# Two PSUM banks for the side chain and two for the maxima's ring, in a planned four-network kernel

## The reference, cut to what matters

```python
# L0, non-local block: keys and values are 2x2 max-pooled, 256 of them
f = softmax(einsum('bcn,bcm->bnm', theta(x), pool(phi(x))))          # 1024 x 256
x = bn(conv1x1(einsum('bnm,bcm->bcn', f, pool(g(x))))) + x
# L1, wavelet block: Haar transform, 1x1 convolutions, spatial and channel gates
x = haar_inverse(relu(bn(proj(gates(relu(bn(fuse(haar(x))))))))) + x
# L2, attention with one head over 128 channels
q, k, v = conv1x1(group_norm(x))
alpha = softmax(einsum('bci,bcj->bij', q, k) * C ** -0.5)             # 1024 x 1024
x = x + conv1x1(einsum('bcj,bij->bci', v, alpha))
# L3, attention with eight heads of 16 channels, then a small MLP
q, k, v = split(einsum('oc,bchw->bohw', w_qkv, group_norm(x)))
attn = softmax(einsum('bhdi,bhdj->bhij', q, k) * temp)                # 8 x 1024 x 1024
x = x + conv1x1(einsum('bhdj,bhij->bhdi', v, attn))
x = x + mlp(group_norm(x))
```

## Time and profile before

| | |
|---|---|
| median of 3 runs | 1871.0 us (1866.97 to 1877.07) |
| profiled execution, own time / span | 1865.36 us / 1863.9 us |
| TensorE (PE) busy | 1565.3 us, 84% of the span |
| VectorE (DVE) busy | 1133.5 us, 61% |
| ScalarE (ACT) busy | 815.9 us, 44% |
| GpSimd (POOL) busy | 273.7 us, 15% |
| granted TensorE clock, mean | 0.871 of full speed |
| one full window (936 to 1149 us) | 213 us |

### The profile page before, as it was taken

The page is one execution under the profiler, slowest core; times in us unless marked ns, Lnnn a source line. Parts: engine busy times, 40 slices in busy tenths (PEclk is TensorE's granted clock), DMA queues, the critical chain, the costliest instruction groups (busy, mean ns, idle before and its releaser), DMA issues.

```text
span 1863.9 us, 20833 instructions
## 1 busy us (share of the span) xinstructions
PE 1565.3 (84%) x6466; PEld 695.4 (37%) x6466; DVE 1133.5 (61%) x1912; ACT 815.9 (44%) x1514; POOL 273.7 (15%) x305
## 2 busy tenths in 40 slices
PE   6579679898889989899889998799879989985982
PEld 3236325433443335333343335333343334332330
DVE  5454664766568584767568574776667574665601
ACT  1113202465327552465327552365326553752670
POOL 5004102110130103010130102201130103000000
PEclk6789957998889799899889799898899899976995
DMA  2000012011110303011120303003020203023001
GB/s 50 12 12 6 11 29 52 6 26 45 28 37 7 80 1 65 6 29 53 25 41 7 80 1 60 12 7 75 12 53 7 68 11 61 18 52 58 13 12 35
DMA packets 31569, 58.64 MB, mean 31 GB/s; under 512 B 14678, under 2 KB 16862, under 8 KB 31456
## 3 DMA queue, kind: packets, MB, share of 16 engines
q1 hardware_dynamic: 27296, 50.41, 12.6%
q0 software_dynamic: 4160, 6.83, 2.4%
HBM read 14.37 MB, written 4.50 MB: 10 GB/s over the span
## 4 chain that ended last, share of the span: by engine, by line
PE 52%; issue 20%; DVE 8%; DMA 6%; SPq 5%; ACT 4%; POOL 3%; POOLq 0%; ACTq 0%; DVEq 0%
PE ps L1337 52%; SPq L689 3%; DVE x L1189 3%; DVE mx L1283 3%; DMA invw<-inverse_sums 2%; DMA qp<-q3h 2%; POOL acc L849 2%; ACT p L1015 2%; SPq L666 1%; SPq L692 1%; POOL ogc L816 1%; DMA inverse_sums<-inv 1%; ACT hn L928 0%; DVE x L1196 0%; DVE x L1195 0%
## 5 line engine op out<-in xcount | busy, mean ns | idle before, releaser
L1283 DVE TENSOR_REDUCE mx<-ps 128x1 f32<-128x512 f32 x1024 | 648.8, 682 | 259.6 <-PE ps L1337 257.5
L1015 ACT ACTIVATE p<-ps 128x512 f32<-128x512 f32 x1024 | 550.7, 600 | 304.6 <-PE ps L1337 302.5
L1337 PE MATMUL ps<-kp,qp 63*128 63x512 f32 x1024 | 418.2, 512 | 85.2 <-DVE mx L1283 41.4
L1337 PE MATMUL ps<-qp,kp 64*128 64x512 f32 x1024 | 396.5, 478 | 22.5 <-ACT p L1015 17.7
L1337 PEld LDWEIGHTS ps<-qp,kp 64*128 64x128 f32 x1024 | 172.3, 198 | 330.0 <-ACT p L1015 233.5
L1337 PE MATMUL ps<-p,vt 128*32 128x512 f32 x2048 | 287.9, 635 | 6.5 <-ACT p L1015 6.2
L1337 PEld LDWEIGHTS ps<-kp,qp 63*128 63x128 f32 x1024 | 176.2, 206 | 216.8 <-DVE mx L1283 133.8
L980 ACT ACTIVATE p<-ps 128x512 f32<-128x512 f32 x128 | 76.2, 597 | 220.5 <-PE ps L1337 188.3
L1337 PE MATMUL ps<-p,vT 128*128 128x512 f32 x256 | 143.5, 654 | 0.7 <-ACT p L980 0.5
L849 POOL TENSOR_TENSOR acc<-acc,p 128x512 f32<-128x512 f32 x96 | 126.4, 1316 | 70.8 <-ACT p L980 67.3
L1279 DVE TENSOR_REDUCE mx<-ps 128x1 f32<-128x512 f32 x128 | 84.4, 683 | 39.1 <-PE ps L1337 39.1
(11 more groups left out here) (192 smaller groups left out, 1660.3 us busy)
## 6 DMA issues: line engine op xcount, KB each, us to landing
qp<-q3h SPq DMA_DIRECT2D x128, 64.0 KB, 2.9
xin<-in_x SPq DMA_DIRECT2D x8, 512.0 KB, 4.6
acc<-inverse_sums SPq DMA_DIRECT2D x16, 256.0 KB, 3.7
kp<-k3h POOLq DMA_DIRECT2D x64, 64.0 KB, 4.1
qp<-q3l SPq DMA_DIRECT2D x64, 64.0 KB, 3.2
x3a<-x SPq DMA_DIRECT2D x8, 512.0 KB, 4.7
kp<-k3h SPq DMA_DIRECT2D x64, 64.0 KB, 2.5
x3b<-x3a SPq DMA_DIRECT2D x8, 512.0 KB, 2.9
```

Source lines behind the costliest of these rows:

```text
L1015: a.activation(p3[:, s % 2, i, :], ps[:, SB + (u + 1) % 3, :], ACT.Exp).then_inc(sem("p3_ready"), 1)
L1283: v.tensor_reduce(mx3[:, i, c, h:h + 1], ps[:, bank, :], AX.X, ALU.max).then_inc(sem("mx3_ready"), 1)
L1337: return nc.tensor.matmul(o, l, r, start=start, stop=stop)
```

## The change

Three things change together. The maxima's ring in the windows has two banks in place of three (banks 0 and 1). The bank that it gives up, bank 2, becomes the side chain's second bank: `side_bank` gives half 0 to bank 7 and half 1 to bank 2. TensorE then issues both halves of a stage at one visit, and between stages waits for the half in question and not for both. The first part keeps its order (`alone`). The plan's tables are moved by a few laps (the first hunks below are of STEADY: the turns of the maxima, L0 on TensorE and on VectorE, Q2 and Q3 on ScalarE), and the first part gets filler matmuls in laps 9, 10 and 135.

```diff
-    "turned": {"DVE": (69, 87, 157), "PE": (71, 87, 157), "ACT": (71, 89, 158), "SP": (72, 90, 158)},
+    "turned": {"DVE": (69, 83, 157), "PE": (71, 87, 157), "ACT": (71, 88, 158), "SP": (72, 90, 158)},
...
-            "L0": {0: 107, 2: 110, 4: 111, 6: 114, 8: 118, 10: 119, 12: 122, 14: 126, 16: 130, 19: 135, 21: 138, 23: 142, 25: 146, 27: 152, 29: 155, 31: 156, 33: 157},
+            "L0": {0: 107, 2: 110, 4: 111, 6: 114, 8: 118, 10: 119, 12: 122, 14: 126, 16: 130, 19: 135, 21: 138, 23: 141, 25: 145, 27: 152, 29: 157, 31: 158, 33: 163},
...
-            "L0": {5: 111, 7: 114, 9: 117, 11: 119, 13: 122, 15: 126, 28: 152, 30: 155, 32: 157, 34: 158},
+            "L0": {5: 111, 7: 114, 9: 117, 11: 119, 13: 122, 15: 126, 28: 152, 30: 157, 32: 159, 34: 160},
...
-            "Q2": {4: 16, 6: 20, 8: 23, 10: 27, 12: 31, 14: 34, 16: 38},
-            "Q3": {4: 47, 6: 50, 8: 57, 10: 61, 12: 65, 14: 69, 16: 74},
+            "Q2": {4: 16, 6: 20, 8: 23, 10: 25, 12: 29, 14: 32, 16: 36},
+            "Q3": {4: 47, 6: 50, 8: 57, 10: 59, 12: 65, 14: 69, 16: 71},
...
-STEADY_PLAN = Plan(STEADY, (1, None, 0), 3)
-LAST_PLAN = Plan(LAST, (1, None, 0), 3)
+STEADY_PLAN = Plan(STEADY, (1, None, 0), 2)
+LAST_PLAN = Plan(LAST, (1, None, 0), 2)
...
+        def side_bank(at, k, first=XB):
+
+            return first if at.plan is FIRST_PLAN else (XB, MB + 2)[k % 2]
...
                 for name, w, n, before in ((q, wq, 5, None), (k, wk, 9, q)):
                     for h in range(NH):
-                        yield at(bt, stage, n + 2 * h)
-                        if h:
+                        alone = at.plan is FIRST_PLAN
+                        if alone or h == 0:
+                            yield at(bt, stage, n + 2 * h)
+                        if alone and h:
                             wait(pe, sem(name + "_split"), bt, NH, h)
                         elif before:
-                            wait(pe, sem(before + "_split"), bt, NH)
-                        else:
+                            wait(pe, sem(before + "_split"), bt, NH, NH if alone else h + 1)
+                        elif h == 0:
                             wait(pe, sem("h" + tag + "_ready"), bt)
-                        mm(ps[:, XB, :], w, half(hn, h)).then_inc(sem(name + "_ps"), 1)
+                        mm(ps[:, side_bank(at, h), :], w, half(hn, h)).then_inc(sem(name + "_ps"), 1)
...
                 for h in range(NH):
-                    yield at(bt, "L0", 27 + 2 * h)
-                    if h:
+                    if alone or h == 0:
+                        yield at(bt, "L0", 27 + 2 * h)
+                    if alone and h:
                         wait(pe, sem("inv0_ready"), bt, NH, h)
-                    else:
+                    elif h == 0:
                         wait(pe, sem("p0_added"), bt)
-                    mm(ps[:, bank_of(bt), :], ones[:], half(x1, h)).then_inc(sem("den0_ps"), 1)
+                    mm(ps[:, side_bank(at, h, MB + 2), :], ones[:], half(x1, h)).then_inc(sem("den0_ps"), 1)
                 for h in range(NH):
-                    yield at(bt, "L0", 31 + 2 * h)
-                    if h:
+                    if alone or h == 0:
+                        yield at(bt, "L0", 31 + 2 * h)
+                    if alone and h:
                         wait(pe, sem("x1_ready"), bt, NH, h)
                     else:
-                        wait(pe, sem("inv0_ready"), bt, NH)
+                        wait(pe, sem("inv0_ready"), bt, NH, NH if alone else h + 1)
                     for m in range(2):
-                        last = mm(ps[:, bank_of(bt), :], wg[:, m, :], half(p0[:, m, :], h), start=m == 0, stop=m == 1)
+                        last = mm(ps[:, side_bank(at, h, MB + 2), :], wg[:, m, :], half(p0[:, m, :], h), start=m == 0, stop=m == 1)
                     last.then_inc(sem("y0_ps"), 1)
...
```

More of the change, by code:

```diff
@@ L243 @@
     "fill": "000000000000000000000000000000000000000000000000000000000000000000000000000000000000000000000000000000000000000000000000000000000000000000000000000000000000000000000000000000000000",
-    "beside": 73,
+    "beside": 72,
 }
@@ L939, in queries @@
                         wait(act, sem(name + "_ps"), bt, NH, h + 1)
-                        a.activation(half(hi, h), ps[:, XB, :], ACT.Identity, bias=bias).then_inc(sem(name + "_hi"), 1)
+                        a.activation(half(hi, h), ps[:, side_bank(at, h), :], ACT.Identity, bias=bias).then_inc(sem(name + "_hi"), 1)
                 for h in range(NH):
@@ L955, in projections @@
                         wait(act, sem(name + "_ps"), bt, NH, h + 1)
[L956 removed]
+                        a.activation(half(hi, h), ps[:, side_bank(at, h), :], ACT.Copy, scale=scale).then_inc(sem(name + "_hi"), 1)
                 for h in range(NH):
@@ L1188, in non_local @@
                     wait(dve, sem("den0_ps"), bt, NH, h + 1)
-                    v.reciprocal(half(x1, h), ps[:, bank_of(bt), :]).then_inc(sem("inv0_ready"), 1)
+                    v.reciprocal(half(x1, h), ps[:, side_bank(at, h, MB + 2), :]).then_inc(sem("inv0_ready"), 1)
                 for h in range(NH):
@@ L1404, in non_local @@
                 wait(pe, sem("x_in"), bt, 16)
+                alone = at.plan is FIRST_PLAN
                 for h in range(NH):
-                    yield at(bt, "L0", 2 * h)
-                    if h:
+                    if alone or h == 0:
+                        yield at(bt, "L0", 2 * h)
+                    if alone and h:
                         wait(pe, sem("theta_ready"), bt, NH, h)
-                    mm(ps[0:CI, bank_of(bt), :], wth[:], half(xin, h)).then_inc(sem("theta_ps"), 1)
+                    mm(ps[0:CI, side_bank(at, h, MB + 2), :], wth[:], half(xin, h)).then_inc(sem("theta_ps"), 1)
                 for h in range(NH):
-                    yield at(bt, "L0", 4 + 2 * h)
-                    if h:
+                    if alone or h == 0:
+                        yield at(bt, "L0", 4 + 2 * h)
+                    if alone and h:
                         wait(pe, sem("pooled"), bt, NH, h)
                     else:
-                        wait(pe, sem("theta_ready"), bt, NH)
-                    mm(ps[:, bank_of(bt), :], wpg[:], half(xin, h)).then_inc(sem("phig_ps"), 1)
+                        wait(pe, sem("theta_ready"), bt, NH, NH if alone else h + 1)
+                    mm(ps[:, side_bank(at, h, MB + 2), :], wpg[:], half(xin, h)).then_inc(sem("phig_ps"), 1)
                 for k in range(4):
-                    yield at(bt, "L0", 8 + 2 * k)
-                    if k:
-                        wait(pe, sem("nm0_ready"), bt, 4, k)
-                    else:
+                    if alone or k % 2 == 0:
+                        yield at(bt, "L0", 8 + 2 * k)
+                    if k == 0:
                         wait(pe, sem("phi_ready"), bt, 2)
+                    elif alone or k >= 2:
+                        wait(pe, sem("nm0_ready"), bt, 4, k if alone else k - 1)
                     for c in (2 * k, 2 * k + 1):
-                        last = mm(ps[:, bank_of(bt), M0 * (c % 2):M0 * (c % 2 + 1)], part(th, c), phz[:])
+                        last = mm(ps[:, side_bank(at, k, MB + 2), M0 * (c % 2):M0 * (c % 2 + 1)], part(th, c), phz[:])
                     last.then_inc(sem("s0max_ps"), 1)
@@ L1495, in wavelet @@
                 for k in range(4):
-                    if k % 2 == 0:
+                    alone = at.plan is FIRST_PLAN
+                    if k == 0 or alone and k == 2:
                         yield at(bt, "L1", 13 + k)
-                        if k:
-                            wait(pe, sem("pj_ready"), bt, 4, k)
-                        else:
-                            wait(pe, sem("chout_ready"), bt)
-                    last = mm(ps[:, XB, Q * (k % 2):Q * (k % 2 + 1)], part(wpr, k), chout[:])
+                    if k == 0:
+                        wait(pe, sem("chout_ready"), bt)
+                    elif alone and k == 2:
+                        wait(pe, sem("pj_ready"), bt, 4, k)
+                    last = mm(ps[:, side_bank(at, k // 2), Q * (k % 2):Q * (k % 2 + 1)], part(wpr, k), chout[:])
                     if k % 2:
@@ L1557, in tail @@
                 for h in range(NH):
-                    yield at(bt, "TL", 2 * h)
-                    if h:
-                        wait(pe, sem("x4_ready"), bt, NH, h)
-                    else:
+                    if h == 0:
+                        yield at(bt, "TL", 2 * h)
                         wait(pe, sem("yn_ready"), bt)
@@ L1564, in tail @@
                         wait(pe, sem("xo_ready"), bt + -1, NH)
-                    mm(ps[:, XB, :], wo[:], half(ogc, h)).then_inc(sem("o3_ps"), 1)
+                    mm(ps[:, side_bank(at, h), :], wo[:], half(ogc, h)).then_inc(sem("o3_ps"), 1)
                 yield from group_averages("TL", 4, bt, grp4, "4", mv4, ps[:, XB, 0:1], ps[:, XB, 1:2])
@@ L1573, in tail @@
                 for h in range(NH):
```

(8 more changed lines are left out.)

73 lines of the change are left out of this document (38 added, 35 removed), and 10 rows, old and new, of tables (FIRST, LAST, STEADY).

## The result

The changed kernel takes 1979.82 us (median of 4 runs, 1976.51 to 1982.78); the kernel before beside it 1868.99 (4 runs). The ratio is 1.060, interval 1.0569 to 1.0631: 111 us slower. The profiled execution of after took 1976.51, its span is 1974.9, its mean granted clock 0.874 (before: span 1863.9, 0.871).

A forecast was written before the change was run, and what follows sets the result against it. TensorE was taken to set the pace, with the three-bank ring's latency at its limit in each burst. 100 - 20 - 11 + 10 + 4 + 17 = +100 on 1865.36 gave 1965, forecast as 1971 us at the median; range 1878 to 2070.

The forecast's parts named there:

- The burst: Heads, burst without side work: with two banks the fourth maxima tile starts 0.60 us late, so 2.73 becomes 3.33 us.
- 154 bursts at 0.65 = 100: Heads: 154 bursts between value products each pay 0.65 us for the two-bank ring, 100 us in all.
- The 28 bursts that were taken off: Heads: of 182 bursts, 28 (four a window) were held free of loss because paired side visits cover the wait.
- the bound: Heads: upper limit of the ring's price, 182 bursts at 0.75 us, 137 us.
- What the pairs cost, +10: Two halves at one visit fill the wait for ScalarE once, not twice: 0.4 us more per pair, +10 us.
- their waits, -11: Side chain: TensorE's waits for v's copies and k's low parts go, and some in the last tail: -11 us.
- End of L0, -20: Ends of five windows: both sums come at once, the next window begins 4 us sooner, -20 us.
- The one wait for a reciprocal that was to stay before y: End of L0: of TensorE's waits for L1189, all were to go but one before y.
- Moved visits, +4: STEADY laps 27, 34 and 61: ScalarE's earlier reads of k and v delay exponentials, +4 us.
- Clock, +17: Heads before L0 begins: in half of six windows four bursts stay at half clock, +17 us.
- The rival in which the clock falls for good: Heads: gaps of 0.6 us keep half of the 154 bursts at half clock, 2050 to 2080 us; chance 0.2.
- The third bank is not needed: Rival, heads: the 0.60 runs beside ScalarE's wait at the fourth score tile, only pairs count, 1845 us; chance 0.09.

The follow-up runs named there:

- the ring alone: The kernel before with only the windows' maxima ring cut from three banks to two, side chain and tables kept: 2072.37 us, ratio 1.1118.

## Why the prediction was right, and which of its terms were not

The direction, the mechanism and the total were right: slower by 111 us where 100 were forecast, 1979.8 against 1971. The total owes something to luck: errors of both signs cancel in it.

- *The burst.* Right. 3.31 us came where 3.33 was worked out, with the third tile 0.06 after the reduction two places before. A visit after tile 2 does cover the wait, as the pair of 4.25 us shows.
- *154 bursts at 0.65 = 100.* Too small for the ring alone, which costs 208 us, 161 of them in the heads. The 28 bursts that were taken off are covered by pairs, so the ring alone stands against 182 x 0.65 = 118. The prediction priced a burst with a visit between tiles 3 and 4 at 0.75 and kept it for the bound; it is 0.83 to 0.85 in the table of the four bursts, and such bursts are common. The third stretch of a window pays 2.8, for side work in front of a reduction, which had no term. Up to about 47 of the 161 us can be clock. In the kernel after, the heads and the step between them cost 109 us in all.
- *Attention part.* A term that was missing. The ring runs into VectorE's wavelet block earlier: +27 us in the profile. Moving two tiles gives 21 us back, but a like move gives the kernel before 17. The bursts in the prediction were counted in the heads only.
- *What the pairs cost, +10, and their waits, -11.* The net of the two was forecast at about nothing, and with the -20 at L0's ends all pairs stood at -21. The runs give -82: L0's ends are 25 us below the kernel before and 33 below the ring alone, and in the heads the pairs give 41 back, some of the 82 by the clock. The step reckoned the pairs against bursts of three banks, where a half fills the wait for ScalarE. In the ring of two banks a half after tile 3 hides 0.13 us of itself, and a pair after tile 2 nearly 1 us: 3.31 + 1.94 (a pair ahead of the tiles: 5.25 - 3.31) - 4.25 = 1.00.
- *End of L0, -20.* Right in size: -22 in the profile, in five windows. The one wait for a reciprocal that was to stay before y did not: at the window's end TensorE now waits for the ring and the turn, and the 9.7 us for L1193 lie in the first part.
- *Moved visits, +4.* Wrong sign, small: the tables together give about 10 us back. In five windows the pair moved to lap 141 gives 0.8 each, 4 in all.
- *Clock, +17.* Not seen as a loss of its own: the mean is 0.874 against 0.871. The rival in which the clock falls for good is out. The first group of heads, at 1.00 before in windows 0 to 6, is at 1.00 after in windows 1 to 6; in the one of 65.7 us it has nine recorded gaps of 0.19 to 1.12 us. What the Trainium skill tells of a bf16 kernel ("TensorE: Matmul & The Clock Gate", section "A second HAM failure mode: psum-queue depth-cycling"), that small idle gaps send the clock back and forth, is therefore not borne out in these groups of the kernel after. The ring alone comes nearer to it: in windows 0 to 5 the same groups fall to 0.50 once, for 3.4 to 13.6 us, and its mean over the span is 0.850. The first part, where the prediction saw agreement, stays at 0.50 for 35 us and does not go back and forth.
- *The third bank is not needed.* Out: ScalarE's wait does not run beside the 0.60, as the waits for it fell from 23.9 us to 10.7 while the bursts grew.

Full windows take 227 us (224 forecast).

## What to carry to other kernels

Count a ring's banks against the latency of its loop in the burst that sets the pace, not against the consumer's load: VectorE was idle for over a third of the time, and the third bank was worth 208 us alone, up to about 70 of them by a lower clock. When a bank is wanted elsewhere, look first for one that is empty at that moment (the ring's own at a window's end, another after its copy) before taking one for good. Price a taken bank with the fillers in place, since work that hid in the old wait shows again, and look for the consumer's longest block everywhere in the loop, not in the inner burst alone.

## What the runs showed of the hardware

A wait for a bank ends 0.06 us after the reduction that frees it, in the kernel before and after. With two banks a pair ahead of the tiles lengthens a burst by 1.94 us, two halves in two places by 5.28 - 3.30 = 1.98: grouping four side matmuls saves next to nothing by itself. A group of heads with nine recorded gaps of 0.19 to 1.12 us kept the granted clock at 1.00, its upper level, for 66 us. In the ring alone it was 0.50 for 6.8 us behind a wait of 1.67 us. The attention part, with its wait of 7.31 us, had 0.85.
